# Fourteen products of a block of zeros on TensorE during the first loads of a post-norm transformer layer

## What is computed

```python
q, k, v = (x @ W.T + b for W, b in ((Wq, bq), (Wk, bk), (Wv, bv)))   # reshaped to 16 heads of 32
q, k = rope(q), rope(k)
qk  = einsum('bshd,bstd->bsht', q, k) / sqrt(32)     # the heads of one position against each other
out = einsum('bsht,bstd->bshd', softmax(qk), v)
out = swapaxes(out, 1, 2).reshape(B, S, E) @ Wo.T + bo
x   = layernorm(x + out)
g, u = (x @ gate_w.T) * gate_s, (x @ up_w.T) * up_s   # 512 -> 1408, ternary weights
x   = layernorm(x + (silu(g) * u) @ down_w.T * down_s)
```

## Time and profile before

| | |
|---|---|
| median of the runs | 1772.54 us (1771.85, 1772.54, 1773.41) |
| the profiled execution: its time, its span | 1772.76 us, 1771.0 us |
| mean granted TensorE clock | 0.991 of 2.4 GHz |
| TensorE products, share of the span | 97% |
| VectorE, ScalarE, GpSimd | 78%, 53%, 46% |
| attention phase / feed-forward phase | to about 850 us / from there |
| first product of TensorE | 8.05 us after the start of the span |

### The profile page before, as it was taken

The page is one execution under the profiler, slowest core; times in us unless marked ns, Lnnn a source line. Parts: engine busy times, 40 slices in busy tenths (PEclk is TensorE's granted clock), DMA queues, the critical chain, the costliest instruction groups (busy, mean ns, idle before and its releaser), DMA issues.

```text
span 1771.0 us, 40772 instructions
## 1 busy us (share of the span) xinstructions
PE 1714.1 (97%) x15138; PEld 1402.4 (79%) x15138; DVE 1384.8 (78%) x1980; ACT 942.4 (53%) x1457; POOL 813.2 (46%) x697
## 2 busy tenths in 40 slices
PE   8799999999999999999799999999999999999997
PEld 6677888888888888888578888888888888888886
DVE  7788999998999999999756766677676776767756
ACT  4445545545654555565535455554555545555453
POOL 6778888888888888889200110201102011020112
PEclk9899999999999999999899999999999999999999
DMA  7367776787677767868774452643526445264251
GB/s 211 84 147 172 161 178 167 154 178 176 161 152 178 171 159 168 178 162 189 199 244 134 134 168 83 206 151 133 170 80 206 151 133 172 79 205 151 87 184 63
DMA packets 447191, 278.06 MB, mean 157 GB/s; under 512 B 261408, under 2 KB 385696, under 8 KB 447136
## 3 DMA queue, kind: packets, MB, share of 16 engines
q1 hardware_dynamic: 447136, 277.37, 58.5%
HBM read 183.97 MB, written 93.32 MB: 157 GB/s over the span
## 4 chain that ended last, share of the span: by engine, by line
PE 91%; DVE 3%; issue 3%; ACT 1%; POOL 1%; SPq 1%; DMA 0%; POOLq 0%; ACTq 0%; DVEq 0%
PE ps_x L615 12%; PE ps_x L619 12%; PE ps_x L616 12%; PE ps_s L778 9%; PE ps_s L783 8%; PE ps_x L778 7%; PE ps_x L783 7%; PE ps_x L789 4%; PE ps_x L793 4%; PE ps_s L691 3%; PE ps_a L649 2%; PE ps_a L793 2%; PE ps_a L789 2%; PE ps_s L789 2%; PE ps_s L793 2%
## 5 line engine op out<-in xcount | busy, mean ns | idle before, releaser
L615 PE MATMUL ps_x<-wqkv_hi,xc_hi 128*128 128x512 f32 x768 | 304.4, 396 | 18.8 <-POOL xc_lo L1162 11.0
L616 PE MATMUL ps_x<-wqkv_lo,xc_hi 128*128 128x512 f32 x768 | 300.9, 392 | 0.0
L619 PE MATMUL ps_x<-wqkv_hi,xc_lo 128*128 128x512 f32 x768 | 300.7, 392 | 0.0
L1298 POOL TENSOR_TENSOR z<-z,xr 128x512 f32<-128x512 f32 x60 | 77.2, 1311 | 482.8 <-DVE z L1631 482.8
L778 PE MATMUL ps_s<-x_hi,slot 128*128 128x512 f32 x672 | 264.9, 394 | 3.1 <-DVE hid L1564 2.1
L783 PE MATMUL ps_s<-x_lo,slot 128*128 128x512 f32 x672 | 262.1, 390 | 0.0
L932 ACT ACTIVATE kX<-kT 32x512 f32<-32x512 f32 x256 | 160.8, 628 | 167.9 <-DVE kT L1383 165.6
L1184 POOL TENSOR_TENSOR qk_cos<-qk_in,rot 128x512 f32<-128x512 f32 x128 | 202.7, 1584 | 74.3 <-DVE qk_in L1360 54.7
L778 PE MATMUL ps_x<-x_hi,slot 128*128 128x512 f32 x560 | 220.0, 393 | 10.6 <-issue 7.9
L783 PE MATMUL ps_x<-x_lo,slot 128*128 128x512 f32 x560 | 218.9, 391 | 0.0
L1190 POOL TENSOR_TENSOR qk_cos<-qk_cos,qk_sin 128x512 f32<-128x512 f32 x128 | 204.2, 1596 | 14.2 <-DVE qk_sin L1367 4.3
(11 more groups left out here) (117 smaller groups left out, 3733.8 us busy)
## 6 DMA issues: line engine op xcount, KB each, us to landing
slot<-gu_hi SPq DMA_DIRECT2D x88, 896.0 KB, 5.1
xc<-x_cols SPq DMA_DIRECT2D x32, 512.0 KB, 5.4
v_rows<-v_in SPq DMA_DIRECT2D x32, 512.0 KB, 4.3
v<-v_rows SPq DMA_DIRECT2D x32, 512.0 KB, 5.2
res<-x_rows SPq DMA_DIRECT2D x64, 256.0 KB, 3.8
x_rows<-x_out SPq DMA_DIRECT2D x32, 512.0 KB, 2.9
x_cols<-x_turn SPq DMA_DIRECT2D x128, 128.0 KB, 2.6
wide<-x_cols SPq DMA_DIRECT2D x64, 256.0 KB, 5.1
```

The lines of the kernel that those rows point to most:

```text
L615: pe.matmul(out, hi[:, k], w_hi[w][:, k], start=(k == 0), stop=False)
L616: pe.matmul(out, hi[:, k], w_lo[w][:, k], start=False, stop=False)
L619: last = pe.matmul(out, lo[:, k], w_hi[w][:, k], start=False, stop=(k == KE - 1))
L1298: pool.tensor_tensor(z[:, h, r], z[:, h, r], rows_of_x1(n, h)[:, r], ALU.add).then_inc(z_added[h], 1)
```

## The change

A constant `WARM` of 14 and a semaphore `warm_set` are added. GpSimd, ahead of its first subtraction, sets `aT_hi[:, 0]` (128 x 512) to zero and signals. TensorE, ahead of `project_qk(0, 0)`, waits for that signal and then makes fourteen products of 128x128 by 128x512 with `aT_hi[:, 0, 0]` as the weights and the whole of `aT_hi[:, 0]` as the moving operand, each into `ps_a[:, 0]` with a start and a stop of its own. Nothing reads these results, and nothing waits for them but what follows in TensorE's own program.

```diff
+WARM = 14
...
+        warm_set = sem("warm_set")
...
+            pe.wait_ge(warm_set, 1)
+            for _ in range(WARM):
+                pe.matmul(ps_a[:, 0], aT_hi[:, 0, 0], aT_hi[:, 0].rearrange("p b x -> p (b x)"), start=True, stop=True)
             project_qk(0, 0)
             project_qk(0, 1)
             project_v(0)
...
+            pool.memset(aT_hi[:, 0].bitcast(F32), 0.0).then_inc(warm_set, 1)
             low_x(0, 0)
             low_x(0, 1)
```

## The result

The changed kernel takes 1777.54 us, the median of 15 runs (1770.84 to 1782.19), against 1772.62 us for the kernel before in the same comparison (15 runs, 1771.20 to 1774.37). The ratio is 1.0025, with an interval of 1.0018 to 1.0032: slower by 4.9 us. The forecast was 1772.6 with a range up to 1775.8, and 0.92 for no difference; it missed, and on the side to which it had given 0.05. The runs after lie 11 us apart, those of before 3 us. The profiled execution of after took 1779.26 us, with a span of 1775.8.

What follows compares the result with a forecast made beforehand. TensorE looked like the bound overall, but the start was bound by a chain of waits avoiding TensorE until 22.87 us. Terms 0 + 0 + 0 + 0 left the time unchanged: forecast 1772.6 us, range 1770.7 to 1775.8.

Steps and rivals of the forecast that it cites:

- The bound of the start: Until 22.87 us the chain of waits does not pass through TensorE, which waits for VectorE's V low parts.
- The clearing and the fourteen products: At the start, clearing takes 0.44 us and products run from about 1.3 to 7.4 us, hidden before 8.05: 0.
- Absorption: K and Q products end 1.6 us earlier, but TensorE then waits for V low parts until 22.87: 0; chance 0.50.
- The full saving: Rival: the first twelve products' faster clock counts in full, 2.4 us off, 1770.1 us; chance 0.05.
- The clock at the new gap: Rival: the clock falls after TensorE's gaps between 19.9 and 22.87 us, costing 1.2 us, 1773.7; chance 0.27.
- The longer program: 29 added TensorE instructions shift unexplained gaps, read as code loads, in the hand-written stretch: 0, plus or minus 1.2 us.
- the prediction's own sign: The prediction is wrong if the gaps of 60 to 150 us change by over 3 us in sum.
- The rival of the code shift: Rival: the 1.38 us gap between 79 and 121 us grows, or others appear: 1773.7 us; chance 0.08 either way.
- The count of 29 instructions: At TensorE's start: 14 multiplications, 14 weight loads and one wait, ahead of everything.

Runs made afterwards that it cites:

- experiment 2: Changed kernel without its fourteen products, GpSimd's clearing, signal and TensorE's wait kept: 1773.30 us, ratio 1.0002.
- experiment 5: Flag turned round and the two branch bodies swapped on TensorE and SyncE: 1768.11 us on the kernel before, 1766.80 on the changed one; repeats 1768.18 and 1768.20.

## Why the prediction was wrong, and where it was right

**The bound of the start, right.** TensorE was taken for the one that waits up to 22.87 us, with VectorE's V low parts as its releaser. It still waits for them: 21.40 (predicted 21.1) and 23.09 (22.87), released by VectorE both times.

**The clearing and the fourteen products, right.** 0.52 us (0.44 taken); start 1.32 (1.3), end 6.75 (up to 7.4), ahead of the 7.89 of the real work. The wait alone measured as nothing (experiment 2).

**Absorption, right.** 2.4 us of faster products end in two longer waits, and the loop's product stands at 791.99 against 792.02. The full saving, a rival at 0.05, fell.

**The clock at the new gap.** In the profile of after no stretch of lower clock stands between 22 and 49 us. But the mechanism is real: in one of the five profiles that have these products at full size the clock fell there. The windows of the changed kernel with its branches changed about, first profile:

```profile
19.00:22.90 3.90, 2.10 (x9) 1.11 (x7) 3.90 (x4) 3.16 (x5) 3.26 (x2) 1.00 0.79 275
22.90:26.30 3.40, 3.27 (x8) 2.62 (x9) 3.08 (x5) 0.00 (x0) 1.53 (x1) 0.50 0.04 6
```

and its `split_x`:

```profile
26.96 0.63 ACT L920 ACTIVATE xc_hi<-xc 128x512 fp32r<-128x512 f32 x1 [4.59 <-PE ps_x L621]
```

That is 1.5 us behind the 25.48 of after; the price had been put at 1.2. It was the slowest of that kernel's six runs, 1769.56 us. One profile in five is too few to judge the chance of 0.27 by. It may be part of the scatter of these kernels; it is no part of the 4.3 us behind the jump.

**The longer program: here it failed.** The step said "I take 0, between the two, and keep plus and minus 1.2 for the range", and it looked at the gaps between 79 and 121 us only. Two things in it were right: that such gaps are code being loaded, and that added instructions move or remove them. In the hand-written stretch the three gaps of the earlier trace rows are gone in after. What the engine saved there it stood elsewhere: 6.44 us ahead of 80.66 (5.28 ahead of 79.45 before), 1.50 ahead of 106.31 (0.65 ahead of 108.00) and 4.71 ahead of 137.78 (1.08 ahead of 139.04), each time ahead of the same product as before. None of these products stands at an edge, which speaks for waits that the profile does not name and against loads of code. In sum it cost nothing, as taken, since the loop's product kept its time, and the prediction's own sign, a change of over 3 us in the gaps of 60 to 150 us, did not come: TensorE's gaps of over half a microsecond there are 12.7 us before and 13.4 after. What was left out is the place where the loads of code were not ahead of the engine: behind the jump over `products(True)`. The trace of before showed it, with 7.94 us put down to "issue" ahead of 858.26, the longest such gap of the whole timeline, but the step goes no further than 121 us. The term there measured +4.3 us in the profile, and the whole +4.9 us in the runs, against a bound of 1.2. The rival of the code shift had the right mechanism, with the wrong place, a price of 1.2 and a chance of 0.08. The count of 29 instructions was one too high.

The Trainium skill, "Runtime: NRT & Kernel Launch", section "Instruction fetch mechanics", says that crossing a block is mostly hidden. I let that stand beside the zero. This case has both sides: in sequence it is hidden among the large products of experiment 5, but not in or beside the runs of small products of the earlier trace rows, where edges stand with 1.78, 1.38 and 1.16 us; and behind the jump it cost 3.35 us in after. The same section warns that "Branching breaks sequential prefetch"; the 7.94 us ahead of the jump's first product, which fall to 2.66 when the jump goes, agree with it. I had cited the one sentence without weighing the other.

Still open: what sets the moment at which the second load starts. From the first product behind the jump it took 1.8 to 3.8 us over the six profiles of the table, and 4.18 to 6.48 until the block was usable. The DMA engines are 0.95 busy from 858 to 864 us in after, so the load of the code may stand behind data; that was not tried. The split of the loss into gap and slower products is read from the profiles and no run separates the two. With fourteen dead products it is the same as in after: 11.13 us from 857.57 to 868.70 against the 7.01 of before, 2.81 of it the gap and 1.3 the slower products. With ten it is 3.0 us in all, though the span is 6.1 us longer, so half of the loss of that execution lies elsewhere and is not explained.

## What to carry to other kernels

Every instruction added ahead of a jump, run or not, moves the code behind it against the blocks in which it is loaded, and that can cost more than the edit's own work: compare such an edit also with an equal number of instructions in a branch that is never taken, and see in the compiled program that the padding is still there. Look in the timeline for gaps put down to "issue" over the whole span, above all behind branches. Put the body that runs directly behind the test, so that the engine goes on in sequence; here that, on TensorE and SyncE together, gave 4.4 us.

## What was not expected

- Products that never run cost 6.5 us (1778.95 against 1772.43 us in the same comparison, five runs), no less than the real ones within the scatter.
- The lowest runs of the changed kernel (1770.84) are as fast as those of before (1771.20), and the highest are 8 us above before's highest. The runs of after lie 11 us apart, with ten dead products 8 (7 runs), with the products over 8 columns 7 (12 runs), with fourteen dead ones 3 (5 runs), before 3; what makes them scatter is not shown.
- No-operations do not survive the build.
